# A transformer kernel on one core: raw token transposes moved ahead of weighing and scoring, their copy moved behind the norms

## The reference, cut to what matters

```python
for i in range(6):
    x = attn_layer(shift_tokens(x), Wqkv[i], q_scale[i], k_scale[i], Wo[i]) + x
    x = ffn_layer(shift_tokens(x), ...) + x

def attn_layer(x, Wqkv, qs, ksc, Wo):      # 16 heads of 64, windows of 32 tokens
    q, k, v = split(x @ Wqkv)
    q = rotary(l2norm(q) * qs) * scale     # norms are taken per head and token
    k = rotary(l2norm(k) * ksc) / scale
    # a window's queries see its own 32 keys and the 32 before them
    attn = softmax(8 * q @ k.T, masked)
    return (attn @ v) @ Wo
```

## Time and profile before

| | |
|---|---|
| runs, median (lowest to highest) | 4038.67 us (4036.61 to 4046.14) |
| profiled execution | 4045.71 us, of which span 4044.0 us |
| busy share TensorE, ScalarE, VectorE, GpSimd | 89%, 75%, 69%, 68% |
| mean granted TensorE clock | 0.964 |

### The profile page before, as it was taken

The page is one execution under the profiler, slowest core; times in us unless marked ns, Lnnn a source line. Parts: engine busy times, 40 slices in busy tenths (PEclk is TensorE's granted clock), DMA queues, the critical chain, the costliest instruction groups (busy, mean ns, idle before and its releaser), DMA issues.

```text
span 4044.0 us, 94657 instructions
## 1 busy us (share of the span) xinstructions
PE 3594.8 (89%) x30888; PEld 2704.4 (67%) x30894; DVE 2777.7 (69%) x3770; ACT 3018.1 (75%) x6096; POOL 2730.7 (68%) x2889
## 2 busy tenths in 40 slices
PE   6898689999889999889999799999799999799998
PEld 3444367777567776667776577776577776577776
DVE  5566377776677776677776677776677776677766
ACT  3556488886688887688886688886688886688885
POOL 3554378885588884678883678873788873788872
PEclk7999799999899999899999899999899999899999
DMA  4222100000000001000001000001000001000002
GB/s 128 87 87 92 45 2 0 0 0 4 26 2 0 0 0 28 2 2 0 0 0 29 2 1 0 0 0 28 2 1 0 0 0 28 2 1 0 0 1 69
DMA packets 59745, 67.76 MB, mean 17 GB/s; under 512 B 12006, under 2 KB 40164, under 8 KB 58468
## 3 DMA queue, kind: packets, MB, share of 16 engines
q1 hardware_dynamic: 59492, 64.64, 5.5%
HBM read 46.27 MB, written 18.35 MB: 16 GB/s over the span
## 4 chain that ended last, share of the span: by engine, by line
PE 35%; issue 28%; POOL 22%; ACT 9%; DVE 2%; DMA 1%; POOLq 1%; ACTq 0%; SPq 0%; DVEq 0%
PE bank L401 28%; POOL sb_area L1519 10%; POOL sb_area L1505 6%; PE bank L614 4%; ACT sb_area L790 4%; ACT sb_area L983 2%; POOL sb_xs L1477 1%; POOL sb_area L1527 1%; PE bank L645 1%; POOL sb_xs L1475 1%; PE bank L673 1%; DVE sb_area L1157 1%; ACT sb_area L940 1%; ACT sb_lnb L952 1%; ACT sb_lnb L949 1%
## 5 line engine op out<-in xcount | busy, mean ns | idle before, releaser
L790 ACT ACTIVATE sb_area<-bank 128x512 f32<-128x512 f32 (+4 forms) x2149 | 1336.7, 649 | 452.3 <-PE bank L614 386.1
L1236 DVE TENSOR_TENSOR sb_area<-bank,sb_rots 128x1024 f32<-128x1024 f32 x768 | 907.6, 1220 | 748.0 <-ACT sb_area L940 743.2
L1505 POOL TENSOR_TENSOR sb_area<-sb_area 128x512 f32<-128x512 f32 x768 | 984.1, 1281 | 378.6 <-DVE sb_area L1236 378.0
L401 PE MATMUL bank<-sb_area 128*64 128x64 f32 (+6 forms) x17104 | 1055.9, 276 | 11.4 <-DMA sb_area<-in_c_crot 3.7
L401 PEld LDWEIGHTS bank<-sb_area 128*64 128x64 f32 (+4 forms) x17104 | 751.7, 147 | 283.9 <-issue 240.5
L1519 POOL TENSOR_TENSOR sb_area<-sb_area,sb_rn 128x512 f32<-128x512 f32 x768 | 784.5, 1042 | 56.3 <-POOL sb_xs L1477 40.8
L614 PE MATMUL bank<-sb_ident,sb_area 128*128 128x128 f32 x3072 | 494.4, 284 | 286.0 <-ACT sb_area L790 182.1
L401 PE MATMUL bank<-sb_area,sb_wvo 128*128 128x256 f32 x3072 | 728.3, 381 | 3.1 <-DVE sb_xT L1291 3.1
L401 PE MATMUL bank<-sb_wqk_hi,sb_xwin 128*128 128x512 f32 x1536 | 608.1, 437 | 43.9 <-POOL sb_xwin L1484 38.9
L614 PEld LDWEIGHTS bank<-sb_ident,sb_area 128*128 128x128 f32 x3072 | 342.0, 142 | 439.3 <-POOL sb_area L1519 180.5
L401 PEld LDWEIGHTS bank<-sb_area,sb_wvo 128*128 128x128 f32 x3072 | 555.0, 190 | 75.2 <-issue 8.8
(11 more groups left out here) (115 smaller groups left out, 4103.9 us busy)
## 6 DMA issues: line engine op xcount, KB each, us to landing
qk_rows<-sb_p SPq DMA_DIRECT2D x52, 256.0 KB, 4.2
sb_wqk_hi<-qk_rows SPq DMA_DIRECT2D x32, 256.0 KB, 2.9
sb_wqk_lo<-qk_rows SPq DMA_DIRECT2D x32, 256.0 KB, 2.7
sb_area<-in_Wqkv SPq DMA_DIRECT2D x7, 1024.0 KB, 5.8
sb_area<-in_WvT SPq DMA_DIRECT2D x7, 512.0 KB, 7.5
sb_wo_bd<-in_Wo SPq DMA_DIRECT2D x14, 256.0 KB, 8.5
sb_area<-in_x SPq DMA_DIRECT2D x4, 512.0 KB, 6.1
sb_area<-in_x SPq DMA_DIRECT2D x8, 256.0 KB, 2.9
```

What stands on the lines that cost most here:

```text
L401: return nc.tensor.matmul(o, a, b, start=start, stop=stop, skip_group_check=True)
L790: return nc.scalar.activation(o, i, ACT.Copy)
L1236: tt_(t12[:, c % 2, :, :].rearrange("p u (h d) -> p u h d", h=8), src, bc(rots[:, tt, s, :, :], [P, 2, 8, D], 2), ALU.mult).then_inc(S["ro ...
L1505: pt_(qn[:, c, :].rearrange("p (h e d) -> p h e d", h=8, e=2), t12[:, c % 2, 0, :].rearrange("p (h e d) -> p h e d", h=8, e=2), swapped, A ...
```

## The change

On TensorE `windows()` is called ahead of `weigh` and `score` instead of behind them. On ScalarE the copy of its result is called behind `norms` and ahead of `turned_p` and `weighed`, instead of behind those. No instruction is added or removed. On VectorE, GpSimd and SP nothing changes.

```diff
@@ TensorE @@
                         turn_p(wp)
+                        if wp == 1:
+                            windows()
                         weigh(4 - wp, 1 - wp)
                         score(wp)
-                        if wp == 1:
-                            windows()
                         turn_qk(2 * wp + 1)
                         project_out(wp)
@@ ScalarE @@
                         norms(1 - wp, 1 - wp)
+                        if wp == 1:
+                            windows()
                         turned_p(wp)
                         weighed(4 - wp, 1 - wp)
-                        if wp == 1:
-                            windows()
-                        elif not (part == 0 and t == 0) and (v := behind(t, i, part, -1)):
+                        if wp == 0 and not (part == 0 and t == 0) and (v := behind(t, i, part, -1)):
                             heads_of_tokens(*v)
                         turned_qk(2 * wp + 1)
```

## The result

The changed kernel took 3910.06 us (median of 4 runs, 3905.78 to 3916.98) against 4037.64 us for the kernel before (4036.18 to 4046.14): ratio 0.9681, 95% interval 0.966 to 0.9702. It is 128 us faster. The forecast was 3859 us, with a range of 3838 to 3918: the sign and the wait that goes were right, the size was 179 us forecast for 128 measured, and the time lies at rival 1 (3910). It lies above the forecast's own worked-out bounds (3843 to 3894); the range holds it because its top was drawn to take in rival 1.

A forecast was written before the change was run, and what follows sets the result against it. No engine is full; a cross-engine chain bounds the kernel, with TensorE's `turn_qk(3)` waiting for ScalarE's third copy. Six layers gaining 30.0 each save 180: 4045.7 - 180 = 3865.7, less 7.0 to the median, 3859 us; range 3838 to 3918.

The forecast's parts named there:

- the sign: Whole kernel: faster by over 0.3%, chance 0.92; within 0.3%, 0.05; slower, 0.03.
- rival 1: GpSimd's load starts 0.2 us late or operations stretch, holding `turn_qk(0)`: gain 0.72 a step, 3910 us; chance 0.14.
- worked-out bounds: Whole kernel: 1.06 a step and 0.8 per odd one gives 3843; 0.86 and 0.2 gives 3894.
- The wait at `turn_qk(3)`: TensorE's 0.86 us idle for ScalarE's third copy goes altogether; `turn_qk(3)` starts 1.04 us earlier.
- V + 4.80: Forecast start of `turn_qk(3)` on TensorE, counted from V, the start of `turn_qk(2)`.
- ScalarE and VectorE behind it: Mask ends near 1510.05, not 1510.49, freeing ScalarE by 0.45; VectorE's 0.48 cover takes the scores' 0.26 delay.
- GpSimd's load: `load_next()` loses its 0.64 us idle, starts 1507.42 to 1507.72; TensorE is let go between 1509.73 and 1510.03.
- the V half: From `turn_qk(2)` to the next step's `turn_qk(0)`, wp = 1: 8.04 us before, ending 0.90 to 1.04 earlier.
- The U half: From `turn_qk(0)` to the next `turn_qk(2)`, wp = 0, starting at U: set by ScalarE, keeps 7.11 us.
- the slack: TensorE's 0.38 us ahead of `turn_qk(2)` takes in `turn_p(0)` waiting up to 0.30 for GpSimd's `normalise`.
- The sum: 27 full steps of 1.02 plus 2.5 gives 30.0 a layer, 180 for six; loop turn near 56.6 us.
- Rivals 2 to 4: ScalarE paces whole step, 4038; transposes delay scores, 4110; `turn_qk(3)` held by scaled chunk. Chances 0.05 (2 and 4), 0.03.

The follow-up runs named there:

- the last kernel: Changed kernel with load_next behind normalise, ScalarE's heads_of_tokens behind turned_qk(1), and turned_qk(1) ahead of weighed in the wp = 0 half: 3767.69 us, ratio 0.9328.

## Why the prediction was right, and where it was off

- *The wait at `turn_qk(3)`.* Right, and nearly to the size: V + 4.80 was worked out, V + 4.77 measured; `windows()` took 0.32 and `turn_p` ahead of it 0.43 where 0.26 and 0.53 stood in the sum. That it was a wait for the third copy, and not for the transposes, is shown by the halves of the change: 0 us for earlier transposes alone, 36 for an earlier copy alone, 128 together.
- *ScalarE and VectorE behind it.* Right. The mask now waits 0.40 for VectorE's subtraction, and `turned_qk(0)` still waits for TensorE behind it.
- *GpSimd's load.* Here is the term that was mis-sized. I let it start at 1507.42 to 1507.72, that is 0.05 ahead to 0.25 behind the end of the addition, and took a place near the early end. It starts 0.32 behind. The trace before hid this wait, since the one on `xwt` ended later; but it stood in the code: `load_next` waits for a count of `add` that only the addition just issued can bring, a trip through the semaphore on the same engine. I had its duration bounded by the reaction to another engine (0.25), which is less. GpSimd's waits on its own last instruction could be seen in the earlier trace rows too: the scaling there stands 0.24 behind the load. With 0.32 the chain of the prediction gives (1470.24 - 1465.65) + 0.32 + 1.21 + 1.02 + 0.08 = 7.22 for the V half; 7.21 was measured.
- *The U half.* 7.11 was forecast, 7.18 measured. ScalarE takes up `turned_qk(0)` 0.69 after its transposes start, and 0.63 in the kernel before; the four transposes of `turn_qk(0)` are shown 0.66 long where it had to wait and 0.60 where TensorE came straight to them. With the load moved they are 0.60 again, and the U half is back at 7.12. That `turn_p(0)` would be late is right (1474.86, U + 2.00, for U + 1.83 before), and also that the slack takes it in.
- *The loop's first step.* It is 14.66 where the others are 14.39 (15.29, and 15.09 to 15.16, in the kernel before), with an idle behind line 1519. The prediction had no term for it. It goes to 14.23 against 14.11 when the load is moved, so some 0.15 of the 0.27 is on GpSimd's path. What GpSimd does more there the runs don't tell. In the last kernel, where TensorE sets the pace, the first step is as long as the others.
- *The sum.* 57.82 - 56.6 = 1.2 us a turn is 44 of the 51 us by which the forecast was off; the load's place accounts for 1.26 of a turn and 63 us in all. So what happened is rival 1's mechanism, through its first condition (the load starts too late); its second, stretched operations, did not: they have the lengths of the earlier trace rows. That its 3910 us came out to the microsecond is in part luck. It took the load to start 0.2 us behind the bounds and the V half to be 7.3; the load was 0.07 behind the later bound and the V half 7.21, and the rest was made up by the longer U half and the loop's first step, for which it had no terms.
- *Rivals 2 to 4.* None. ScalarE's busy time in a turn was 50.74 and is 50.52, and the turn fell by 2.87. The Trainium skill ("Perfetto Trace Analysis", Identifying the Most-Contended Engine) judges TensorE by its weight loads (or by its share of peak FLOPs, not worked out here) and says to work first on the engine with the highest occupancy. By that ScalarE comes ahead of TensorE in every kernel here: 84% of the turn to 74% before, 91% to 83% in the last one. The runs disagree for this kernel: it was shortened by order alone, with ScalarE's work left as it is, down to a turn whose length is that of TensorE's matmuls.

## What to carry to other kernels

A result that sits third in another engine's queue is late however early its input is made: move producer and consumer together, and test the halves apart. When a wait on a far engine is taken away, look up in the code which waits stand beside it, those on the same engine too, and give them a duration: they are what is late next, and a wait on one's own last instruction cost 0.32 us here, 54 us in all. Once the chain is known in halves, each queue that crosses it can be put in order one by one, and the gains add, as they did here (55.75 us for 55.77), as long as another engine doesn't take over. Read waits of a fraction of a microsecond on TensorE from starts, not from its idle.

## What I had not expected of the hardware

- On GpSimd, waiting for its own preceding addition puts 0.32 us between the two instructions; without the wait the next one starts 0.04 ahead of the recorded end (1.24 after the start of one that is 1.28 long). Two other waits of GpSimd on its own last instruction stand beside it with 0.18 and 0.24 us.
- The releaser that the profile names can be off where two engines end within 0.1 us of each other: it named line 1519 for `turn_qk(2)`, and moving a ScalarE instruction of 0.3 us out of the way moved `turn_qk(2)` by 0.2 while line 1519 ended after it.
- TensorE's shown busy time filled a loop turn of 54.84 us wholly, with the granted clock at 1.00 (2.4 GHz), as in the kernel before at 93% busy. The busy time of the same matmuls was between 54.84 and 57.10 us a turn, depending on the waits around them.
